# Two moves in TensorE's instruction order: a group of transpositions ahead of the state update, the mask product ahead of a gate projection

## The reference, cut to what matters

```
# stage 1: retention, 8 heads, decay_h per head
q, k, v = split(x @ w_qkv.T)                 # 256, 256, 512 columns
q, k = xpos(q), xpos(k)                      # rotation with position tables
out[t] = sum over s <= t of (q_t . k_s) * scale * decay_h ** (t - s) * v_s
normed = per-head normalisation of out       # 64 columns a head
y = (silu(x @ w_gated.T) * normed) @ w_proj.T
x = layernorm(x + y)
# stage 2: feed-forward with FP4 quantise-dequantise of every operand, 704 wide
x = layernorm(x + fp4_linear(silu(fp4_linear(x, w_gate)) * fp4_linear(x, w_up), w_down))
```

## Time and profile before

| | |
|---|---|
| Median of 3 runs | 580.21 us (580.19 to 580.23) |
| The profiled execution's own time | 580.19 us |
| Its span in the profile | 578.4 us |
| Mean granted TensorE clock | 0.994 of full speed |
| PE busy | 560.5 us, 97% of the span |
| PE weight loads busy | 485.5 us, 84% |
| DVE busy | 514.3 us, 89% |
| ACT busy | 337.2 us, 58% |
| POOL busy | 228.6 us, 40% |

### The profile page before, as it was taken

How to read it: one execution, slowest core, us unless ns; L and a number is a source line. 1 busy time by engine, 2 the same in 40 slices (tenths; PEclk the granted TensorE clock), 3 DMA queues, 4 the chain that set the end, 5 groups by cost and what they waited for, 6 DMA issues and landing times.

```text
span 578.4 us, 14053 instructions
## 1 busy us (share of the span) xinstructions
PE 560.5 (97%) x4432; PEld 485.5 (84%) x4432; DVE 514.3 (89%) x1283; ACT 337.2 (58%) x818; POOL 228.6 (40%) x260
## 2 busy tenths in 40 slices
PE   7999999999999999999999999999999999999984
PEld 4788888888888888888888788889999999999984
DVE  7667878999999999999999899999999999888896
ACT  4455766776686676768667744434445545445342
POOL 3211121435334353533434224555654655644420
PEclk9999999999999999999999999999999999999988
DMA  6700110110111011011101000000010100000002
GB/s 209 227 34 29 56 47 12 56 54 22 33 54 45 9 54 54 7 47 54 38 17 36 20 19 1 1 0 2 1 38 1 38 20 19 19 19 19 19 19 92
DMA packets 24983, 22.32 MB, mean 39 GB/s; under 512 B 2025, under 2 KB 21874, under 8 KB 24946
## 3 DMA queue, kind: packets, MB, share of 16 engines
q1 hardware_dynamic: 24130, 20.27, 11.5%
q10 hardware_dynamic: 816, 1.57, 0.8%
HBM read 17.63 MB, written 4.20 MB: 38 GB/s over the span
## 4 chain that ended last, share of the span: by engine, by line
PE 84%; DVE 7%; issue 4%; POOL 3%; ACT 1%; DMA 1%; ACTq 0%; DVEq 0%; POOLq 0%
PE wide_banks L1364 57%; PE wide_banks L1435 9%; PE wide_banks L1412 4%; PE wide_banks L1552 3%; PE wide_banks L1423 3%; PE turn L1461 3%; PE turn L1398 2%; PE wide_banks L1448 2%; DVE shared L854 1%; POOL shared L1325 1%; PE turn L1561 1%; DVE shared L859 1%; DVE shared L676 1%; POOL shared L1330 1%; DMA x<-in_w_in 1%
## 5 line engine op out<-in xcount | busy, mean ns | idle before, releaser
L1330 POOL TENSOR_TENSOR shared<-shared,h_scale 128x704 f32<-128x704 bf16 x31 | 43.0, 1389 | 78.4 <-DVE shared L859 76.1
L1364 PE MATMUL wide_banks<-win_hi,x_hi 128*128 128x512 f32 x192 | 65.4, 422 | 3.6 <-DVE win_lo L937 1.8
L1435 PEld LDWEIGHTS wide_banks<-shared 128*128 128x128 f32 x512 | 62.0, 192 | 2.8
L461 ACT ACTIVATE shared<-opened,rstd 128x64 f32<-128x64 f32 x240 | 63.5, 339 | 1.0
L558 ACT ACTIVATE shared<-wide_banks 128x512 f32<-128x512 f32 x64 | 29.6, 462 | 53.7 <-PE wide_banks L1364 53.2
L1435 PE MATMUL wide_banks<-shared 128*128 128x64 f32 x512 | 60.6, 271 | 0.0
L1364 PE MATMUL wide_banks<-win_hi,x_lo 128*128 128x512 f32 x192 | 60.4, 396 | 0.0
L1364 PE MATMUL wide_banks<-win_lo,x_hi 128*128 128x512 f32 x192 | 60.3, 395 | 0.0
L1364 PE MATMUL wide_banks<-wgu_hi,xq_hi 128*128 128x512 f32 (+1 forms) x192 | 59.7, 392 | 0.6 <-DVE xq_lo L1067 0.6
L427 ACT ACTIVATE shared<-shared 128x704 bf16<-128x704 f32 x32 | 25.3, 791 | 54.6 <-POOL shared L1325 52.2
L1364 PE MATMUL wide_banks<-wgu_lo,xq_hi 128*128 128x512 f32 (+1 forms) x192 | 56.5, 375 | 0.0
(11 more groups left out here) (146 smaller groups left out, 1443.8 us busy)
## 6 DMA issues: line engine op xcount, KB each, us to landing
xf<-in_x_feat SPq DMA_DIRECT2D x32, 128.0 KB, 2.3
tab<-in_tables SPq DMA_DIRECT2D x16, 256.0 KB, 2.7
xt<-in_x_tok SPq DMA_DIRECT2D x32, 128.0 KB, 2.1
out<-x SPq DMA_DIRECT2D x32, 128.0 KB, 1.7
x<-in_w_in ACTq DMA_DIRECT2D x3, 512.0 KB, 5.4
w<-in_w_gu SPq DMA_DIRECT2D x1, 1408.0 KB, 8.8
w<-in_w_down SPq DMA_DIRECT2D x1, 704.0 KB, 10.2
wgu_lo<-pow_dram SPq DMA_DIRECT2D x1, 576.0 KB, 4.4
```

Of the source, the lines that this page charges most:

```text
L461: last = act.activation(gated[:, b, cols], opened[:, b, cols], ACT.Copy, scale=rstd[:, b, 1 + k:2 + k])
L1330: pool.tensor_tensor(over_blocks(hq[:, b]), over_blocks(h_steps[:, b]), spread(h_fp4["scale"][:, b]), ALU.mult).then_inc(h_fp4["ready"], 1)
L1364: last = pe.matmul(dst, lhs, rhs, start=k == 0, stop=k == len(parts) - 1)
L1435: last = pe.matmul(mixed[:, r, DV * at:DV * (at + 1)], ret[:, slot(k)], vs[:, b, DV * k:DV * (k + 1)], start=False, stop=k >= HEADS - 2, s ...
```

## The change

In the list of TensorE alone, `turn_gated(n - 3)` moves from behind `cross(n)` to a place ahead of `update(n)`, directly behind `scores(n)`. It applies to all steps that have it, 3 to 31. And `flip_mask`, which is called in step -1 alone, moves from behind `project_gate(0)` to a place directly behind `project_v(0)`. No instruction is added or removed, all waits stay with their instructions, and the other engines' lists are the same.

```diff
@@ -1480,16 +1480,18 @@
                     project_qk(n + 1, 1 - b)
                 if valid(n):
                     scores(n)
+                if in_turn(n - LAG):
+                    turn_gated(n - LAG, 1 - b)
                 if carried(n):
                     update(n, b)
                 if valid(n):
                     cross(n, b)
-                if in_turn(n - LAG):
-                    turn_gated(n - LAG, 1 - b)
                 for group in weights(n, 0):
                     turn_weights(group)
                 if valid(n + 1):
                     project_v(n + 1, 1 - b)
+                if isinstance(n, int) and n == -1:
+                    flip_mask()
                 if valid(n):
                     mix(n, b)
                 for group in weights(n, 1):
@@ -1500,8 +1502,6 @@
                     project_out(n - LAG)
                 if valid(n + 1):
                     project_gate(n + 1, 1 - b)
-                if isinstance(n, int) and n == -1:
-                    flip_mask()
```

## The result

The changed kernel takes 585.62 us in the median of four runs (584.76 to 586.58), the kernel before 580.22 us beside it. The ratio is 1.0091, with a 95% interval of 1.0074 to 1.0107. It is slower, and the time lies inside the predicted range, 1.6 us above the predicted value.

What follows compares the result with a forecast made beforehand. TensorE's own list was taken to bound the kernel: 580.2 us, plus 1.4 for the start and 2.4 for the loop, gave 584.0 us, with a range of 582.3 to 586.8 us.

Steps and rivals of the forecast that it cites:

- three changed hand-overs: TensorE's loop step: passages between neighbouring groups that the new order changes, put at 0.61 us against 0.52.
- loop's term: Loop on TensorE: each step 0.09 us longer by one more change of array shape, 27 steps, 2.4 us.
- two bounds: Loop: `project_v` waits for decayed scores, within 0.01 us of TensorE's order; earlier transpositions meet the wait for decayed queries.
- first rival: Loop: transpositions do wait for `decay_q`; 5.1 us more, 589.1 us, or 586.5 at half size; 14% for half or more.
- at its release: Loop: decayed scores release `project_v` 2.16 us behind the first score in step 30, within 0.01 us of TensorE's order.
- The start: TensorE before tile 0: moved mask products wait for their transfer, so tile 0's transpositions start 1.4 us later.
- third rival: Start: mask data land before TensorE asks, so the start gains 0.3 us; 582.3 us, 4%.
- second rival: Start: idle time of 1.7 us is followed by half clock, losing 1.7 us more; 585.7 us, 10%.

Runs made afterwards that it cites:

- halved transpositions: Against the kernel before: two of the four transpositions moved behind the scores, the other two behind the update; 587.89 us, ratio 1.0125.
- two later profiles: The changed kernel profiled twice more without an edit; both executions took 584.79 and 584.94 us.
- upper place: The 10 of 24 timed executions of the changed kernel that took 586.4 to 586.8 us.
- lower one: The 13 of 24 timed executions of the changed kernel that took 584.5 to 584.9 us.
- longer wait: Against the kernel before: mask products alone moved, waiting also for the four transfers behind theirs; 583.66 us, ratio 1.0058.

## Why the prediction was right, and where its sizes were off

**What bounds the loop.** TensorE does. The step grew by what TensorE's list grew by, in every kernel whose transpositions came in time, and VectorE's idle time grew beside it.

**The price of a seam.** The three changed hand-overs were put at 0.61 us against 0.52. In the trace after they are 148.81 less the last score's start (148.16 + 0.73 - 0.27 = 148.62), 0.19 to 0.20; 149.40 less 149.19, 0.21; and 150.40 less 150.20, 0.20. The estimate held to a hundredth. The halved transpositions and those behind the update then show that it is a price per change of shape: one change more made a step 0.11 us longer in the change and 0.16 with the halves. The Trainium skill (TensorEngine Tiling (Array Packing), Tiling Modes, Key Properties) says that a change of tiling mode drains TensorE. The traces agree with it by the longer hand-overs; a drain itself has no row in them.

**The size of the loop's term.** 27 x 0.09 = 2.4 was predicted, 3.0 measured. The missing 0.03 a step sits in `project_v`. Behind the full-width transpositions its second product came 0.305 us behind the first; behind the cross products it comes 0.338 behind, here and in the variant behind the update (0.340). I had let the groups keep their lengths. Why it is slower there was not tried. With the transpositions behind `project_v`, where `project_v` starts after a wait, it is 0.305 to 0.311, though cross products come before it there too.

**The two bounds.** The transpositions do not wait for `decay_q`, except for 0.03 us in the even tiles, where the group then runs 0.03 shorter. The first rival is out, for the reason given: VectorE, freed of its 0.27, comes earlier by as much. The claim that `project_v` is at its release was right too: in step 30 it is released as before and that step kept its 9.58 us. Step 31 hid less than assumed: the last matmul is 0.12 us later than the shift of that step's scores. Its transpositions now carry the wait for `decay_q` (0.28 us, where the cross products had 0.19). I did not follow that tenth further, and its cause is open.

**The start.** 1.4 was predicted and 1.16 measured. The data landed at 9.2 + 4.5 = 13.7 in this execution against 13.9; that is 0.2 of it. Against the same 15.84 the two later profiles give 1.44 and 1.71, so the forecast lies within what the landing makes of it, and its size in one execution is partly luck. The third rival's gain of 0.3 was undersized. The end of `project_v` in the trace of before:

```profile
11.61 0.63 PE L1364 MATMUL wide_banks<-win_hi,x_lo 128*128 128x512 f32 x2
```

Its last product starts at 11.61 + 0.63 - 0.40 = 11.84, and it is 15.84 - 11.84 = 4.00 us from there to tile 0's transpositions. Where the mask products need no transfer it is 14.98 - 11.63 = 3.35, 0.65 less. The first mask product starts 0.24 behind that last start. In the rows of before this would be 12.08 and not 12.23: I had taken the modelled end of the product for the moment from which TensorE could go on. That is 0.15 of the 0.35 missing. The mask products and the gate projection then take 14.98 - 11.87 = 3.11, where I had counted on 1.71 + 0.11 + 1.48 = 3.30; that is the rest. The kernel measures 0.7 us faster than before.

**The second rival.** It was given 10% and takes place in two of five executions (10 of 24). Its price was right: the upper place is 1.7 us above the lower one. The rows of before had shown one idle time with a fall behind it and one without, and I leaned on the one without. What is shown: the two places come with the moved mask products (both alone and with the loop's change), go when idle products fill the wait, and the runs at the upper place have a mean clock lower by 0.003, which is 1.7 us of the span at 2.4 GHz lost, as much as their time is longer. The kernel before is not quite free of such runs: one of its 49 timed executions took 581.75 us at 0.992, 1.1 above the usual. What is only argued: that the half-speed stretch, 1.2 GHz, lies directly behind the wait; no profile of a run at the upper place was caught. Two things in other profiles speak for it. With the transpositions behind `project_v` a half-speed stretch of 3.4 us lies behind idle times of 1.49 and 0.66 us, so idle time of this size can be enough. And near the end, where TensorE always stands idle for 2.08 or 2.09 us, half speed begins around the end of that idle time (0.2 us before it to 1.4 us behind it) in 8 of the 14 profiled executions and not in the other 6. So the outcome differs from run to run behind the same idle time, and 10% was too low. The Trainium skill (TensorE: Matmul & The Clock Gate, Part 1) says that the moment at which the clock changes, there its rise, differs from run to run. That some executions here show a fall and others none agrees with it; the page gives no chance for a fall.

Taken together, the lower place is at 584.5 to 584.9 us against 584.0 forecast, from + 0.6 in the loop, - 0.2 at the start and + 0.1 at its end. The median of 585.6 lies above it because of the second rival.

## What to carry to other kernels

Where a matrix engine has no gap left, sort its groups by array shape before anything else: each seam between shapes costs, here 0.11 to 0.16 us a step for one more, and a group of the array's full width belongs next to another one. Place a group by who reads its result in order: too early costs a seam, too late can put the reader's whole list behind it and make the two engines wait for each other in turn, and the second was thirteen times dearer here (38.1 us over the kernel before, against 2.9). Behind every product moved ahead of others look up the landing of its data, and count an idle time at the start twice, once as time and once as a chance for the clock to fall.

## What the runs showed of the hardware that was not expected

- The hand-over to another shape of the array was set by the group in front and not by which shape came next. In the nine neighbourhoods of the kernels without a wait it was 0.200 to 0.203 us behind products of 128 columns (scores, cross products, transpositions), 0.149 to 0.150 behind the update's 64 columns and 0.327 behind a projection's 512 (medians). Against the 0.109 between two transpositions and the 0.236 between two projection products this is 0.09 more.
- Behind a change of shape the second transposition came 0.164 to 0.166 us after the first, elsewhere 0.109. A group between two other shapes pays on both sides.
- A projection product directly behind 64-row products was followed by the next one after 0.338 us, behind full-width transpositions after 0.305.
- The mean clock differs between executions of one kernel though their times agree: 0.994 to 0.996 for the transpositions alone, all within 0.35 us. In the 14 profiles it goes with a stretch of 3.4 us at half speed near the end, which eight have (mean 0.992 to 0.995) and six have not (0.995 to 0.996). Beside the kernel with the transpositions behind `project_v`, only runs with 0.990 to 0.992 were clearly longer, with one exception at 0.993 (584.64 us with the longer wait).
- A store of 9 KB issued at 4.1 us was answered only at 9.2 to 9.9 in the profiles with 0.3 MB of loads ahead of it in SyncE's list, and still only at 8.7 in the one without them.
